# A graph layer on one core: ACT, not SP, issues the loads of the weights and of the last nodes

## The chip, the cores and the metric

The kernel runs on one core of a Trainium2 chip. The metric is the device time in microseconds of one execution, the median of several runs.

## What is computed

N is 5000 nodes, F is 64 features, everything in float32. `x` is [5000, 64], `adj` is [5000, 5000] (100 MB, mostly zeros but stored in full), `fc_w` is [64, 128].

```
h = jnp.maximum(_layernorm(x, axis=-1), 0.0)
neighbors = (adj @ h) / (num_neighbors[:, None] + 1e-7)
out = x + relu(concatenate([h, neighbors], -1) @ fc_w.T + fc_b)
```

## The kernel before

The product with `adj` is reordered: the kernel first computes g = h @ (the half of `fc_w` that belongs to the neighbours), and then adj @ g, so that the large product has 64 output features. The transpose of `adj` lies in memory in three groups of columns, 5, 4 and 1 blocks of 512 (the last one shorter). `LOADS` lists 38 loads in order: group by group, and in a group 512 rows of it at a time (4 tiles of 128 rows), which in group 0 is 128 partitions of 4 x 2560 floats, that is 5,120 KB and a contiguous run of 40,960 bytes on each partition. They go into one ring in SBUF, `raw` (32,768 floats a partition). Three loads of group 0 fit in it. `load(n)` on SP waits with `load_used` until PE has used up what lay in the place.

**PE** (`tensor_program`) does in this order: waits for the bias (`bias_loaded`) and spreads it over the partitions (line 683); `turn(0)` transposes the first 1024 normalized nodes (line 576); waits for both weight loads (`weights_loaded`, 32); `weigh(0)` multiplies them with the weights (line 588); then for each load: waits for its landing, and multiplies it (line 627). A tile of group 0 is 12 matrix instructions, a load 48. A set of 8 tiles of g (`g_sb`) is needed before its rows of `adj`; `turn(b)` and `weigh(b)` for the sets 1 to 4 are put between the tiles (`TURN_AFTER`, `WEIGH_AFTER`), the first ones after tile 3 and tile 5. After the last tile of a load `load_used` goes up.

**DVE** clears the parts of tiles that transfers don't fill (`x_cleared`, `weights_cleared`), and then normalizes the nodes in five sets of 8 tiles. The last set needs `x_loaded[1]`, two transfers of the last nodes. Between `normalize(1)` and `normalize(2)` stands `add_bias(0)`, which waits for the bias.

**ACT** warms its table for the square root, then issues `load_few` (the bias, and the few last nodes from partition `PAD0` = 96 on), then the squares and roots of the layer norm, and the copies `ht` and `g_sb` out of PSUM. After the second set it issues the neighbour counts, `load_counts`. It issues on a DMA queue of its own, q10 in the profile; SP's is q1 and POOL's q0.

**POOL** clears `bias_row`, `ones` and other tiles, and loads the eight remaining rows of `adj` (`adj_rem`).

**SP** issues x in two halves (line 257), the tail of x (96 partitions of 1 KB, line 262), waits for `weights_cleared`, issues the weights twice, once for each half of the partitions (line 266, 128 runs of 256 bytes each), and then the 38 loads (line 253). Each load has a semaphore of its own, out of 24.

Of the kernel before, what the change touches and what calls it, by code (L numbers as in the profile page):

```python
# [39 lines left out]
def gnn_layer(nc, x, adj_groups, num_neighbors, fc_t, fc_b, out):  # L40
# [9 lines left out]
    N, F = x.shape  # L50
# [11 lines left out]
    PAD0 = LAST_LANES // 32 * 32  # L62
# [27 lines left out]
    def place(n):  # L90

        g, m, i0, _ = LOADS[n]
        return (RING[g][1] + m * RUN + i0) % RING[g][0] * WIDTH[g]

    def place_end(n):
        return place(n) + (LOADS[n][3] - LOADS[n][2]) * WIDTH[LOADS[n][0]]

    def loads_before(n):

        over = [k + 1 for k in range(n) if place(k) < place_end(n) and place(n) < place_end(k)]  # L100
        return max(over + [n - LANDINGS + 1, 0])
# [13 lines left out]
    with ExitStack() as ctx:  # L115
        def sb(name, shape, dt=F32):
            return ctx.enter_context(nc.sbuf_tensor(name, shape, dt))

        def sem(name):
            return ctx.enter_context(nc.semaphore(name))  # L120
# [3 lines left out]
        x_sb = sb("x_sb", [LANES, TILES, F])  # L124
# [15 lines left out]
        w_both = sb("w_both", [2 * F, 2, 2 * F])  # L140
# [20 lines left out]
        x_loaded = [sem("x_loaded_main"), sem("x_loaded_last")]  # L161
        nn_cleared = sem("nn_cleared")
        nn_loaded = sem("nn_loaded")
        weights_cleared = sem("weights_cleared")
        weights_loaded = sem("weights_loaded")
# [34 lines left out]
        def flat(v):  # L200
            return v.rearrange("p t f -> p (t f)")
# [5 lines left out]
        def tail(v):  # L207

            return v[0:LAST_LANES, ROWS:TILES, :].rearrange("p t f -> p (t f)")

        def tail_nodes(v):
            return v[TAIL0:N, :].rearrange("(p t) f -> p (t f)", t=RUN)
# [22 lines left out]
        def weighed_parts(k, part):  # L235

            return y[k][:].rearrange("p (i s q f) -> p i s q f", i=2, s=2, q=2)[:, :, :, part, :]
# [4 lines left out]
        def loaded(n):  # L242
            return landed[n % LANDINGS], 16 * (n // LANDINGS) + 16

        def sync_program(sp):
            def load(n):
                g, m, i0, i1 = LOADS[n]
                w = WIDTH[g]
                if loads_before(n):
                    sp.wait_ge(load_used, loads_before(n))  # L250
                r = RUN if m < FULL else TAIL_RUN
                rows = adj_groups[g][m * BLOCK:m * BLOCK + r * LANES, 0:w].rearrange("(p i) c -> p (i c)", i=r)
                sp.dma_start(raw[:, place(n):place_end(n)], rows[:, i0 * w:i1 * w]).then_inc(loaded(n)[0], 16)  # L253

            def load_x(k):
                r = slice(ROWS // 2 * k, ROWS // 2 * (k + 1))
                sp.dma_start(x_sb[:, r, :], x[0:TAIL0, :].rearrange("(p r) f -> p r f", r=ROWS)[:, r, :]  # L257
                             ).then_inc(x_loaded[0], 16)

            load_x(0)  # L260
            load_x(1)
            sp.dma_start(tail(x_sb)[0:PAD0], tail_nodes(x)[0:PAD0]).then_inc(x_loaded[1], 16)  # L262
            sp.wait_ge(weights_cleared, 1)
            for s in range(2):
                k = slice(s * F, (s + 1) * F)
                sp.dma_start(w_both[k, s, :].rearrange("r (k c) -> r k c", k=2), fc_t.rearrange("(k r) c -> r k c", k=2)  # L266
                             ).then_inc(weights_loaded, 16)
            for n in range(len(LOADS)):
                load(n)

            sp.wait_ge(out_ready, LAST)
            sp.dma_start(out[0:TAIL0, :].rearrange("(p r) f -> p (r f)", r=ROWS), flat(out_sb[:, 0:ROWS, :])
                         ).then_inc(stored, 16)
            sp.wait_ge(stored, 16)
# [44 lines left out]
        def scalar_program(act):  # L319
            def load_few():  # L320

                act.wait_ge(bias_cleared, 1)
                act.dma_start(bias_row[0:1, :], fc_b.rearrange("(a f) -> a f", a=1)).then_inc(bias_loaded, 16)
                act.wait_ge(x_cleared, 1)
                act.dma_start(tail(x_sb)[PAD0:LAST_LANES], tail_nodes(x)[PAD0:LAST_LANES]).then_inc(x_loaded[1], 16)

            def load_counts():
                act.wait_ge(nn_cleared, 1)
                act.dma_start(nn[:, 0:ROWS], num_neighbors[0:TAIL0].rearrange("(p r) -> p r", r=ROWS)
                              ).then_inc(nn_loaded, 16)  # L330
                act.dma_start(nn[0:LAST_LANES, ROWS:TILES],
                              num_neighbors[TAIL0:N].rearrange("(p t) -> p t", t=RUN)).then_inc(nn_loaded, 16)

            def ln_square(b):
                act.wait_ge(ln_dve, LN_OPS * b + 3)
                nc.scalar.activation(sums[0][:], cen[:], ACT.Square).then_inc(ln_act, 1)  # L336

            def ln_std(b):
                act.wait_ge(ln_dve, LN_OPS * b + 5)
                nc.scalar.activation(std[:], var[:], ACT.Sqrt).then_inc(ln_act, 1)  # L340

            def copy_turned(b):
                act.wait_ge(turned_done, b + 1)
                if b >= 2:
                    act.wait_ge(weighed, b - 1)
                if b == SETS - 1:
                    act.wait_ge(rem_cleared, 2)

                    k = turned[HALF:LANES, :].rearrange("k (t p) -> k p t", t=RUN)[:, 0:LAST_LANES, :]
                    nc.scalar.activation(ht_rows[HALF:LANES, :].rearrange("k (p t) -> k p t", t=RUN), k, ACT.Copy)  # L350

                    nc.scalar.activation(
                        ht_rem[HALF:LANES, 0:REM * REM_STEP].rearrange("k (p t z) -> k p t z", t=RUN, z=REM_STEP)[:, :, :, 0],
                        k[:, LAST_LANES - REM // RUN:LAST_LANES, :], ACT.Copy)
                nc.scalar.activation(ht[b % 2][:], turned[:], ACT.Copy).then_inc(turned_copied, 1)  # L355

            def copy_g(b):
                act.wait_ge(weighed, b + 1)
                to = g_sb[:, BT * b:BT * (b + 1), :].rearrange("p (s i) f -> p i s f", s=2)
                for k in range(2):  # L360
                    nc.scalar.activation(to[:, 2 * k:2 * k + 2, :, :], weighed_parts(k, 1), ACT.Copy).then_inc(g_copied, 1)  # L361

            def copy_spread(b):
                act.wait_ge(spread_done, b + 1)
                w = BLOCK if b != ALONE else BLOCK // 2 + SIDE
                nc.scalar.activation(rnn_bc[:, b, 0:w], y[b % 2][:, 0:w], ACT.Copy).then_inc(spread_copied, 1)  # L366


            act.wait_ge(warm_ready, 1)
            nc.scalar.activation(std[:, 0:1], warm[:], ACT.Sqrt)  # L370
            load_few()
            for b in range(SETS):
                ln_square(b)
                ln_std(b)
                if b == 0:
                    copy_turned(0)
                else:
                    copy_g(b - 1)
                    copy_turned(b)
                if b == 1:  # L380
                    load_counts()
            copy_g(SETS - 1)
            for b in range(SETS):
                copy_spread(b)
            act.wait_ge(out_ready, LAST + 1)
            act.dma_start(tail_nodes(out), tail(out_sb)).then_inc(last_stored, 16)
            act.wait_ge(last_stored, 16)
# [181 lines left out]
        def tensor_program(pe):  # L569
# [142 lines left out]
            flip_last()  # L712

        sync_program(nc.sync)
        gpsimd_program(nc.gpsimd)
        scalar_program(nc.scalar)
        vector_program(nc.vector)
        tensor_program(nc.tensor)
# [27 lines left out]
```

## Time and profile before

| | |
|---|---|
| time, median of 3 runs | 246.38 us (246.18 to 246.43) |
| the profiled execution's own time | 246.37 us |
| span of the profile, first to last instruction | 244.9 us |
| PE busy | 202.8 us (83%) |
| DVE, ACT, POOL busy | 41.6, 15.1, 6.7 us |
| moved by DMA | 102.79 MB, mean 420 GB/s |
| chain that ended last | DMA 67%, PE 18%, issue 11% |

The profile is of one execution. Times in it count from its first instruction. PE is TensorE, DVE VectorE, ACT ScalarE, POOL GpSimd; SPq, ACTq and POOLq are the instructions that issue transfers. A DMA share of 1 means that all 16 engines had a packet in hand; large packets are counted in the window in which they begin, so a short window may show more than 1.

### The profile page before, as it was taken

How to read it: one execution, taken by the hardware profiler on the slowest of the kernel's cores; microseconds unless marked ns; L12 is line 12 of the kernel's file. 1: busy time of each engine (PE TensorE's matmuls, PEld its weight loads, DVE VectorE, ACT ScalarE, POOL GpSimd, SP SyncE). 2: the span in 40 equal slices, each digit the busy share in tenths (PEclk: the TensorE clock that was granted, in tenths of full speed). 3: DMA queues.
4: the chain of work that ended last, by engine and by line, in shares of the span. 5: the costliest groups of instructions: out<-in, count | busy, mean ns of one | idle time of the engine just before them, and what ended most of it. 6: DMA issues, size and time to landing. Idle time of an engine off the chain costs nothing.

```text
span 244.9 us, 2438 instructions
## 1 busy us (share of the span) xinstructions
PE 202.8 (83%) x1086; PEld 84.6 (35%) x1086; DVE 41.6 (17%) x102; ACT 15.1 (6%) x34; POOL 6.7 (3%) x18
## 2 busy tenths in 40 slices
PE   0168789997969796998799899898896699888995
PEld 0143234342324332453233333342222233133663
DVE  1752033304400200050000530221000000002311
ACT  2130201201200110010000300000000000000000
POOL 6000100000100000000000000000000000000000
PEclk9999979999999999999999999999999999999999
DMA  9899999999999999999999999999999999999997
GB/s 305 363 435 435 442 420 408 429 428 442 440 429 448 428 438 435 442 435 415 399 437 428 428 431 434 428 428 439 420 439 434 412 431 426 416 421 419 417 405 283
DMA packets 6847, 102.79 MB, mean 420 GB/s; under 512 B 1346, under 2 KB 1934, under 8 KB 3638
## 3 DMA queue, kind: packets, MB, share of 16 engines
q1 hardware_dynamic: 6304, 102.37, 98.4%
q8 instruction: 8, 0.13, 0.2%
q10 hardware_dynamic: 374, 0.12, 0.2%
q0 software_dynamic: 160, 0.16, 0.2%
q14 instruction: 1, 0.01, 0.0%
HBM read 101.37 MB, written 1.28 MB: 419 GB/s over the span
## 4 chain that ended last, share of the span: by engine, by line
DMA 67%; PE 18%; issue 11%; DVE 2%; SPq 2%; DVEq 0%
DMA raw<-adj_group 67%; PE acc L627 16%; DVE rnn_diag L475 1%; PE turned L627 1%; PE y L613 1%; SPq L266 1%; SPq L253 1%; SPq L257 0%; PE y L605 0%; PE turned L576 0%; DVE out_sb L538 0%; DVE rnn_diag L483 0%; DVE rnn_diag L480 0%; SPq L262 0%; PE acc L677 0%
## 5 line engine op out<-in xcount | busy, mean ns | idle before, releaser
L627 PE MATMUL acc<-raw,g_sb 128*64 128x512 f32 (+1 forms) x780 | 157.2, 556 | 26.0 <-DMA raw<-adj_group 26.0
L627 PEld LDWEIGHTS acc<-raw,g_sb 128*64 128x64 f32 x780 | 55.4, 138 | 123.3 <-issue 84.1
L627 PE MATMUL turned<-raw,g_sb 128*64 128x196 f32 x156 | 15.4, 341 | 1.0 <-DMA raw<-adj_group 0.9
L446 DVE TENSOR_TENSOR out_sb<-y,bias 128x128 f32<-128x128 f32 x20 | 4.4, 282 | 55.0 <-ACT g_sb L361 55.0
L504 DVE TENSOR_TENSOR sums<-acc,rnn_bc 128x512 f32<-128x512 f32 x4 | 2.6, 685 | 60.1 <-PE acc L627 58.1
L588 PE MATMUL y<-w_both,ht 128*128 128x256 f32 (+1 forms) x40 | 12.1, 441 | 0.8 <-ACT ht L355 0.8
L627 PEld LDWEIGHTS turned<-raw,g_sb 128*64 128x64 f32 x156 | 10.0, 134 | 6.5 <-DMA raw<-adj_group 4.1
L588 PEld LDWEIGHTS y<-w_both,ht 128*128 128x128 f32 x40 | 8.0, 217 | 3.9 <-issue 2.7
L576 PE MATMUL turned<-ident,h_pairs 128*128 128x128 f32 x20 | 3.7, 315 | 5.1 <-DVE h_pairs L434 5.1
L530 DVE TENSOR_TENSOR out_sb<-y,out_sb 128x512 f32<-128x512 f32 (+1 forms) x5 | 3.2, 638 | 23.4 <-PE y L659 20.2
L422 DVE TENSOR_REDUCE var<-sums 128x8 f32<-128x512 f32 x5 | 3.4, 686 | 19.9 <-ACT sums L336 19.9
L361 ACT ACTIVATE g_sb<-y 128x256 f32<-128x256 f32 x10 | 3.3, 381 | 53.7 <-PE y L588 35.0
L683 PE MATMUL acc<-bias_row,ones 128*128 128x64 f32 x2 | 0.7, 448 | 5.8 <-DMA bias_row<-fc_b 5.8
L475 DVE TENSOR_TENSOR rnn_diag<-ident,rnn 128x512 f32<-128x512 f32 x8 | 5.1, 686 | 0.2 <-PE y L613 0.2
L613 PE MATMUL y<-rnn_diag,ones 128*64 128x512 f32 (+1 forms) x20 | 4.6, 552 | 0.5 <-DVE rnn_diag L475 0.4
L366 ACT ACTIVATE rnn_bc<-y 128x512 f32<-128x512 f32 (+1 forms) x5 | 2.9, 588 | 31.6 <-PE y L613 31.6
L480 DVE TENSOR_TENSOR rnn_diag<-ident_twice,rnn 128x256 f32<-128x256 f32 x1 | 0.4, 426 | 25.6 <-issue 25.6
L576 PEld LDWEIGHTS turned<-ident,h_pairs 128*128 128x128 f32 x20 | 2.4, 156 | 6.8 <-issue 6.8
L355 ACT ACTIVATE ht<-turned 128x512 f32<-128x512 f32 x5 | 3.0, 597 | 23.9 <-PE turned L576 23.9
L411 DVE TENSOR_REDUCE mean<-x_sb 128x8 f32<-128x512 f32 (+1 forms) x6 | 3.4, 587 | 4.9 <-DMA x_sb<-x 4.9
L646 PE MATMUL acc<-adj_rem,g_sb 128*64 128x512 f32 (+1 forms) x20 | 4.2, 550 | 0.0
L290 POOL DMA_DIRECT2D adj_rem<-adj_group x2 | 1.3, 650 | 86.2 <-PE acc L646 61.2
(61 smaller groups left out, 48.9 us busy)
## 6 DMA issues: line engine op xcount, KB each, us to landing
raw<-adj_group SPq DMA_DIRECT2D x9, 5120.0 KB, 27.3
raw<-adj_group SPq DMA_DIRECT2D x7, 4096.0 KB, 27.9
raw<-adj_group SPq DMA_DIRECT2D x4, 2048.0 KB, 29.2
raw<-adj_group SPq DMA_DIRECT2D x7, 784.0 KB, 26.2
raw<-adj_group SPq DMA_DIRECT2D x1, 3840.0 KB, 24.5
raw<-adj_group SPq DMA_DIRECT2D x3, 1024.0 KB, 26.7
raw<-adj_group SPq DMA_DIRECT2D x4, 392.0 KB, 18.9
x_sb<-x SPq DMA_DIRECT2D x2, 576.0 KB, 4.8
```

The source lines that it names most:

```text
L355: nc.scalar.activation(ht[b % 2][:], turned[:], ACT.Copy).then_inc(turned_copied, 1)
L361: nc.scalar.activation(to[:, 2 * k:2 * k + 2, :, :], weighed_parts(k, 1), ACT.Copy).then_inc(g_copied, 1)
L411: last = nc.vector.tensor_reduce(narrow(mean[:]), rows, AX_X, ALU.add)
L422: nc.vector.tensor_reduce(var[:], sums[0][:].rearrange("p (t f) -> p t f", f=F), AX_X, ALU.add).then_inc(ln_dve, 1)
L446: last = nc.vector.tensor_tensor(to[:, 2 * k:2 * k + 2, :], weighed_parts(k, 0)[:, :, s, :], bias[:].unsqueeze(1).to_broadcast([LANES, 2, ...
L475: last = nc.vector.tensor_tensor(split(to[:, s, :]), ident[:].unsqueeze(1).to_broadcast(shape), rnn[:, m + s:ROWS:FULL].unsqueeze(2).to_br ...
L530: nc.vector.tensor_tensor(o, split(y[b % 2][:, 0:RUN * F * (m1 - m0)]), o, ALU.add).then_inc(summed, 1)
L576: last = nc.tensor.transpose(turned[:, c], h_pairs[b % 2][:, c], ident[:])
L588: last = nc.tensor.matmul(weighed_tiles(i)[:, 0:w], ht[b % 2][:, c:c + LANES], flat(w_both[:])[:, 0:w], start=True, stop=True)
L613: last = nc.tensor.matmul(y[b % 2][k, c], ones[:, 0:HALF], r, start=True, stop=True, tile_position=(0, s * HALF))
L627: last = nc.tensor.matmul(acc[b][s * HALF:(s + 1) * HALF, 0:width], g_sb[:, t, :], k, start=g < G - 1 and t == 0, stop=t == CH - 1, tile_p ...
L646: last = nc.tensor.matmul(acc[b][s * HALF:(s + 1) * HALF, 0:width], g_sb[:, CH, :], k, start=g == G - 1, stop=False, tile_position=(0, s * ...
```

## The change

The issue of the tail of x and of the two weight loads goes from SP to ACT, into `load_few`, ahead of the bias and the few last nodes. `load_few` itself goes ahead of ACT's first activation, before which its table is loaded. SP issues the loads of `raw` right behind x. Nothing is computed otherwise.

```diff
--- before.py
+++ after.py
@@ -259,12 +259,6 @@
 
             load_x(0)
             load_x(1)
-            sp.dma_start(tail(x_sb)[0:PAD0], tail_nodes(x)[0:PAD0]).then_inc(x_loaded[1], 16)
-            sp.wait_ge(weights_cleared, 1)
-            for s in range(2):
-                k = slice(s * F, (s + 1) * F)
-                sp.dma_start(w_both[k, s, :].rearrange("r (k c) -> r k c", k=2), fc_t.rearrange("(k r) c -> r k c", k=2)
-                             ).then_inc(weights_loaded, 16)
             for n in range(len(LOADS)):
                 load(n)
 
@@ -319,6 +313,13 @@
         def scalar_program(act):
             def load_few():
 
+
+                act.dma_start(tail(x_sb)[0:PAD0], tail_nodes(x)[0:PAD0]).then_inc(x_loaded[1], 16)
+                act.wait_ge(weights_cleared, 1)
+                for s in range(2):
+                    k = slice(s * F, (s + 1) * F)
+                    act.dma_start(w_both[k, s, :].rearrange("r (k c) -> r k c", k=2),
+                                  fc_t.rearrange("(k r) c -> r k c", k=2)).then_inc(weights_loaded, 16)
                 act.wait_ge(bias_cleared, 1)
                 act.dma_start(bias_row[0:1, :], fc_b.rearrange("(a f) -> a f", a=1)).then_inc(bias_loaded, 16)
                 act.wait_ge(x_cleared, 1)
@@ -366,9 +367,9 @@
                 nc.scalar.activation(rnn_bc[:, b, 0:w], y[b % 2][:, 0:w], ACT.Copy).then_inc(spread_copied, 1)
 
 
+            load_few()
             act.wait_ge(warm_ready, 1)
             nc.scalar.activation(std[:, 0:1], warm[:], ACT.Sqrt)
-            load_few()
             for b in range(SETS):
                 ln_square(b)
                 ln_std(b)
```

## Rows read from the trace of the kernel before

**Rows 1.** Page, span in forty slices: DMA share in tenths, GB/s of each slice.
```profile
DMA  9899999999999999999999999999999999999997
GB/s 305 363 435 435 442 420 408 429 428 442 440 429 448 428 438 435 442 435 415 399 437 428 428 431 434 428 428 439 420 439 434 412 431 426 416 421 419 417 405 283
```

**Rows 2.** Chain that ended last, in order of time: start, length, what.
```profile
4.67 40.31 DMA raw<-adj_group
...
45.02 8.84 PE acc L627 x48
```

**Rows 3.** Waits of SP's queue: total us, times, longest.
```profile
SPq L253 <- PE acc L627: 198.4, 23, 23.2
```

**Rows 4.** Page, DMA queues: packets, MB, share of 16 engines.
```profile
q1 hardware_dynamic: 6304, 102.37, 98.4%
...
q10 hardware_dynamic: 374, 0.12, 0.2%
```

**Rows 5.** Timeline, 0 to 22 us: start, busy us, engine, line, operation.
```profile
0.74 1.28 ACT L370 ACT_TABLE_LOAD   x1 [0.74 <-PEq L739]
...
0.75 0.85 SPq L257 DMA_DIRECT2D x_sb<-x  x2
...
1.37 0.27 DVE L392 MEMSET w_both<- 128x256 f32 x1
...
1.60 0.52 ACTq L323 DMA_DIRECT2D bias_row<-fc_b  x1
...
1.65 0.42 SPq L262 DMA_DIRECT2D x_sb<-x  x1
...
2.12 1.40 SPq L266 DMA_DIRECT2D w_both<-fc_t  x2
...
3.56 1.55 SPq L253 DMA_DIRECT2D raw<-adj_group  x3
...
5.81 0.69 PE L683 MATMUL acc<-bias_row,ones 128*128 128x64 f32 x2 [5.81 <-DMA bias_row<-fc_b]
...
8.28 0.63 ACT L336 ACTIVATE sums<-cen 128x512 f32<-128x512 f32 x1 [6.04 <-DVE cen L418]
...
11.65 1.09 PE L576 MATMUL turned<-ident,h_pairs 128*128 128x128 f32 x4 [5.15 <-DVE h_pairs L434]
...
13.51 3.75 PE L588 MATMUL y<-w_both,ht 128*128 128x256 f32 x8 [0.78 <-ACT ht L355]
...
17.30 0.66 ACT L361 ACTIVATE g_sb<-y 128x256 f32<-128x256 f32 x2 [2.25 <-PE y L588]
...
19.42 2.80 PE L627 MATMUL acc<-raw,g_sb 128*64 128x512 f32 x14 [2.16 <-DMA raw<-adj_group]
```

**Rows 6.** Two windows: busy us by engine, clock, DMA share, GB/s.
```profile
1.50:2.00 0.50, 0.00 (x0) 0.00 (x0) 0.19 (x2) 0.50 (x1) 0.50 (x3) 1.00 1.09 120
2.00:3.00 1.00, 0.00 (x0) 0.00 (x0) 0.00 (x0) 0.23 (x2) 1.00 (x1) 1.00 0.62 152
```

**Rows 7.** DMA queues in the window 2 to 5 us.
```profile
q1 hardware_dynamic: 224, 0.96, 87.2%
```

**Rows 8.** Timeline, 28 to 34 us.
```profile
28.87 0.36 ACTq L329 DMA_DIRECT2D nn<-num_neighbors  x1
```

**Rows 9.** DMA queues in the window 29 to 32.5 us.
```profile
q1 hardware_dynamic: 58, 1.72, 114.1%
```

**Rows 10.** DMA queues in the window 32.5 to 34 us.
```profile
q1 hardware_dynamic: 15, 0.61, 95.5%
...
q10 hardware_dynamic: 16, 0.00, 0.9%
```

**Rows 11.** DMA queues in the window 32.5 to 57 us.
```profile
q10 hardware_dynamic: 256, 0.02, 0.8%
```

**Rows 12.** Timeline of PE, 34 to 140 us.
```profile
37.48 1.99 PE L588 MATMUL y<-w_both,ht 128*128 128x256 f32 x8
```

**Rows 13.** DMA issues by line: count, KB each, median us to landing.
```profile
adj_rem<-adj_group POOLq DMA_DIRECT2D x1, 16.0 KB, 11.7
```

## The prediction

> **What bounds the kernel now.** I read the page's forty slices first, then the chain that ended last, then the waits of SP's queue, and then the opening in small windows. The slices show the 16 DMA engines at nine tenths or more in nearly all of them, at 400 to 448 GB/s after the first two [rows 1]. The chain's longest piece is a load of `raw` in flight for 40.3 us; then 8.84 us of multiplications free its place in the ring [rows 2]. That isn't PE setting the pace: SP waited 198.4 us in all for PE to free places [rows 3] while the engines stayed full with the two loads behind. Three loads of 5,120 KB fit in the ring, one takes about 12.2 us, and PE uses one up in 8.8 us. So the kernel ends when the last byte of `adj` has come. A stall of PE costs nothing until all queued loads have landed; time in which the DMA engines are dry goes one for one to the end. The question is when they start and whether they ever run dry.
>
> **How the queues are served.** The page counts 6304 packets on q1 (SP's queue) and 374 on q10 (ACT's) [rows 4]. I can rebuild both from the program with one packet per contiguous row plus one completion packet per engine used. SP: 38 loads x 144 = 5472, x 288, tail 112, weights 288, output 144: 6304. ACT: counts 144 + 112, bias 2, last nodes 4, last store 112: 374. So a load of `raw` is eight 40,960-byte rows per engine, and the two weight loads are 288 packets: per engine 8 rows of 256 B, a completion, 8 rows, a completion, that is 18 packets.
>
> A row of 40,960 B takes one engine 1.53 us: 102.37 MB in 98.4% of 16 x 244.9 us [rows 4] is 26.6 GB/s an engine, 1.54 us, and the 435 GB/s slices [rows 1] give 1.51.
>
> Small packets of another queue have to be fitted between these. The trace has exactly that case. ACT issues the neighbour counts (256 packets, 16 an engine, some 20 KB) at 28.87 us [rows 8]. From 29 to 32.5 us q10 moves nothing [rows 9]. From 32.5 to 34 us it moves 16 packets beside 15 of q1 [rows 10], one an engine in the time of one big row. Its 256 packets need until the window that ends at 57 us [rows 11]: 24 us for 20 KB. The same shows on POOL's queue, where 16 KB took 11.7 us to land [rows 13]. So on each engine a small queue gets one packet for each packet of SP's, and before the first it waits for what is already lined up.
>
> The Trainium skill (DMA: Bandwidth & Descriptors, Queues, rings and completion order) says the same of the turn, that an engine goes round its queue rows packet by packet, and adds that a packet typically holds 9 to 17 descriptors. By that addition 16 weight rows would go in one or two turns and the change would be nearly free; the trace has one row per packet for these shapes.
>
> **The change, part by part.**
>
> *Removed from SP.* Tail 0.42 us and weights 1.40 us of issue [rows 5]. The first load of `raw` is issued at 1.65 us in place of 3.56, 1.9 us earlier. This isn't 1.9 us of gain, since the engines are busy with x by then. From 2 to 5 us q1 moved 0.96 of x's 1.18 MB [rows 7], so x drains at about 5.4 us, and `raw` rows only stand behind it. What can be gained is idle DMA at the start: a share of 0.62 in the window from 2 to 3 us [rows 6], 0.4 us, if the tail fills them; the weights arrive too late for it. Bounds 0 to 0.5 us of gain (tail and weights, 0.16 MB, are 0.4 us of DMA at 435 GB/s wherever they go); I take 0.3.
>
> *Added to ACT ahead of its table.* Tail at about 0.74 us (0.42), a wait for the weights' clearing (DVE ends it at 1.64 [rows 5]), weights until about 3.1, bias (0.5) until 3.7, last nodes 0.25, then table 1.28 and the warm square root 0.2: done near 5.5. ACT's first real work is at 8.28 [rows 5]. The cover is 2.8 us, so this costs nothing. Behind the wait stand the bias and last nodes, which go out 1.5 us later than now.
>
> *Where the weights stand now.* Before, they were in front of `raw` on the same queue. Now x and the first loads of `raw` are on SP's queue and the weights on ACT's. SP issues `raw` at 1.65, ACT the first weights at about 1.69, while most of x is still queued. In the old trace the bias, issued on ACT at 1.60, has no packet on q10 before 5 us [rows 7], so what arrives then stands behind x. The weights and the first `raw` rows come up together at about 5.4 us and take turns: 18 for the weights, then two for the bias, on one engine. PE waits for the bias first, then for the weights.
>
> A turn is 8/9 of 1.53 us, as every ninth packet of SP is a tiny completion: 1.36 us. Nineteen turns after the first are 25.9 us. The first comes at 5.4 us, or up to 2.6 us later if rows of `raw` are already lined up: the counts waited 3.6 us from issue to the first packet [rows 8, 9], x only about 1.0 [rows 5, 6]. I take half, 1.3, and 0.7 us from the bias's last packet to PE (now PE starts at 5.81 and q10 has no packet before 5 us, so it is at most 0.8 [rows 5, 7]): 5.4 + 1.3 + 25.9 + 0.7 = 33.3, rounded up to 33.5 because the counts' pace was nearer 1.5 us a turn. Bounds 32.0 (nothing ahead) and 36.7 (2.6 ahead at 1.5 us a turn).
>
> *What that does to PE.* Bias product 0.7 us; then from `turn(0)` to the second `g_sb` copy as now, 11.65 to 17.96 us [rows 5], 6.3. DVE and ACT have x ready long before. The first multiplication starts at 33.5 + 7.0 = 40.5 us, in place of 19.42 [rows 5]. Load 0 is used up at 40.5 + 8.8 = 49.3 [rows 2], and only then may SP issue the fourth. Its first packet comes 1.0 us later, at 50.3.
>
> *When the engines run dry.* Three loads are 24 rows an engine, 36.7 us; from 5.4 us, with 0.4 for tail and weights, they end at 42.5. Dry from 42.5 to 50.3: **7.8 us**. No second gap follows: after load 0 PE needs a transposition (some 0.6 us), 8.8 of load 1 and a warm `weigh` of 1.99 [rows 12], 11.4 us, under the 12.2 of the fourth load. This margin is 0.8 us; at half clock that `weigh` takes what `weigh(0)` takes, 3.75 us [rows 5], and 1 us more is lost.
>
> *Sum.* 7.8 - 0.3 = +7.5 us on the profiled execution of 246.37 (span 244.9 and 1.5 around it), which is the median of 246.38: **253.9 us**.
>
> **Rivals.**
>
> A. *The weights pass ahead of `raw`.* If they reach the engines before the first `raw` rows and are taken in at once, or several rows move per turn, or they mix with x's 0.18-us packets, PE starts early enough. The point where it decides: load 0 must be used up by 42.5 - 1.0 = 41.5, so the bias must be seen by 41.5 - 8.8 - 7.0 = 25.7 us, six turns before my figure. For it: ACT's weight issue may begin nearly with SP's, and x is slow until 3 us [rows 6]. Against it: x was wholly lined up in front of the bias, and the counts show one row per turn. Then the time is 246.4 less 0 to 0.5: 246.2. Chance 0.08, nearly all inside 0.2%.
>
> B. *The earlier issue counts* (the other side). With A's condition met, the engines take `raw` 1.9 us earlier in effect or at least fill their 0.5 us idle at the start: 244.5 to 245.9, centre 245.7. The idle share up to 3 us speaks for it, the full share after that against. Chance 0.04.
>
> C. *The same mechanism, larger or smaller.* A few weight rows pass with x, each worth 1.36 us: 248.5 to 251.2 with two to four of them. Or a cold TensorE: if first multiplications run at the 1.2 GHz level, 2 us more, and the second gap 1 us: 257. This is the range of my forecast; its chance with the forecast is 0.88.
>
> **How the numbers follow.** Forecast with C 0.88, all slower; A 0.08; B 0.04. 0.2% of this kernel is 0.5 us, about what can be told from no change. Slower 0.88, same 0.08, faster 0.04. The early bias (32.0) gives 252.4 and the late one (36.7) 257.1; three to four passed weight rows take the low end to 249.0, and the second gap with a late bias the high end to 258.0. A and B are left outside.
>
> **What the new profile would show.** Right: q10 with about 16 packets per 1.5 us from 6 us on; the bias product near 33.5 us and the first product of line 627 near 40.5 (lines as in the kernel before); the weights' landing some 25 to 29 us after issue instead of 4.7; two DMA slices of the forty well below the rest around 43 to 50 us; no idle DMA after that. Wrong: a bias product before 26 us, or DMA slices full throughout. If PE starts at 40 us but the DMA slices stay full, the ring is deeper than I count; if the gap is there but the end doesn't move, the kernel isn't DMA-bound later on.

## The result: 4% slower, and what the profile after shows

The changed kernel takes 256.36 us (median of 6 runs, 255.3 to 257.35), the kernel before 246.31 (median of 6 beside it). The ratio is 1.0405, with a 95% interval of 1.0388 to 1.0423: 10.05 us slower. The forecast was 253.9, in a range of 249.0 to 258.0. The profiled execution took 257.12 us, with a span of 255.7.

Line numbers after line 262 have moved: 627 is now 628, 588 is 589, 576 is 577, 683 is 684.

The page first: its DMA shares and GB/s in forty slices of 6.4 us, where before all slices were full [rows 1], and the packet counts of the queues [rows 4].

```profile
DMA  7999994099999999999999999999999999999996
GB/s 303 413 413 445 458 436 205 0 354 433 418 429 408 438 436 449 419 423 423 445 430 432 420 426 428 446 420 426 438 436 431 418 426 420 423 415 418 420 404 260
...
q1 hardware_dynamic: 5904, 102.20, 94.2%
q10 hardware_dynamic: 774, 0.29, 0.5%
```

The eighth slice, from 44.8 to 51.1 us, moves nothing at all, and the seventh half of what it could. 400 packets have gone from q1 to q10: 112 of the tail and 288 of the weights, as counted.

The timeline from the start, up to the first multiplication of `raw` (compare [rows 5]):

```profile
0.76 0.40 ACTq L317 DMA_DIRECT2D x_sb<-x  x1
...
1.65 49.76 SPq L253 DMA_DIRECT2D raw<-adj_group  x4
1.67 1.37 ACTq L321 DMA_DIRECT2D w_both<-fc_t  x2
3.08 0.73 ACTq L324 DMA_DIRECT2D bias_row<-fc_b  x1
...
4.13 1.28 ACT L372 ACT_TABLE_LOAD   x1 [4.13 <-issue]
...
33.56 0.69 PE L684 MATMUL acc<-bias_row,ones 128*128 128x64 f32 x2 [33.56 <-DMA bias_row<-fc_b]
...
34.05 1.06 PE L577 MATMUL turned<-ident,h_pairs 128*128 128x128 f32 x4
```

```profile
35.89 3.75 PE L589 MATMUL y<-w_both,ht 128*128 128x256 f32 x8 [0.78 <-ACT ht L356]
40.48 10.57 PE L628 MATMUL acc<-raw,g_sb 128*64 128x512 f32 x48 [0.84 <-ACT g_sb L362]
50.98 0.66 PE L577 MATMUL turned<-ident,h_pairs 128*128 128x128 f32 x4
```

SP issues `raw` 1.9 us earlier, as meant, and ACT's table load hides. But PE sits from the start until 33.56 us for a bias of 256 bytes. Its first multiplication of `raw` is at 40.48 us in place of 19.42, and SP can issue the fourth load only after that of load 0 has ended:

```profile
51.08 0.33 SPq L253 DMA_DIRECT2D raw<-adj_group  x1
```

Windows of the same execution (busy us by engine, granted clock, DMA share, GB/s; a packet counts where it begins):

```profile
41.00:42.00 1.00, 1.00 (x4) 0.27 (x2) 0.93 (x4) 0.00 (x0) 0.00 (x0) 1.00 0.67 287
42.00:51.00 9.00, 9.00 (x47) 3.57 (x43) 0.57 (x1) 0.00 (x0) 0.00 (x0) 1.00 0.00 0
51.00:52.00 1.00, 1.00 (x8) 0.59 (x8) 0.00 (x0) 0.33 (x1) 0.00 (x0) 1.00 0.00 0
52.00:53.00 1.00, 1.00 (x8) 0.38 (x6) 0.00 (x0) 0.72 (x2) 0.65 (x1) 1.00 2.26 655
```

No row of `adj` begins between 42 and 52 us. PE is busy in all of it, on data that landed long ago.

What kept the bias is in the queues' packets. First the window 6.5 to 8 us, then 6.5 to 29 us (queue, packets, MB, share):

```profile
q1 hardware_dynamic: 16, 0.66, 101.3%
q10 hardware_dynamic: 16, 0.00, 1.2%
```

```profile
q1 hardware_dynamic: 255, 9.79, 101.7%
q10 hardware_dynamic: 255, 0.06, 1.2%
```

255 packets against 255: one small packet for each packet of SP's. In 22.5 us ACT's queue moves 0.06 MB. It is the pattern of the neighbour counts [rows 9 to 11], at the place where it hurts.

The chain that ended last says it too (start, length, what): where SP's issue and a load stood at its beginning, there is now the bias.

```profile
1.67 0.65 ACTq L321
2.36 0.68 ACTq L321
3.08 30.44 DMA bias_row<-fc_b
33.56 0.69 PE acc L684 x2
34.26 0.87 PE turned L577 x4
```

### The profile page after: what moved, and what is told of

Read it like the earlier page. It is cut to its first block, busy times and chain, and to the rows that moved or that the text cites. A ratio compares the mean times of both kernels' runs of the same rounds, so it can differ in the third digit from the quotient of the medians.

```text
span 255.7 us, 2438 instructions
## 1 busy us (share of the span) xinstructions
PE 205.8 (80%) x1086; PEld 86.0 (34%) x1086; DVE 41.6 (16%) x102; ACT 15.1 (6%) x34; POOL 6.6 (3%) x18
## 4 chain that ended last, share of the span: by engine, by line
DMA 47%; PE 37%; issue 12%; DVE 2%; ACTq 1%; ACT 0%; SPq 0%; DVEq 0%
DMA raw<-adj_group 35%; PE acc L628 30%; DMA bias_row<-fc_b 12%; PE y L589 4%; PE turned L577 1%; DVE rnn_diag L476 1%; PE turned L628 1%; PE y L614 1%; ACTq L321 1%; PE acc L684 0%; PE y L606 0%; ACT g_sb L362 0%; ACT ht L356 0%; DVE out_sb L539 0%; DVE rnn_diag L484 0%
## 5 line engine op out<-in xcount | busy, mean ns | idle before, releaser
L628 PE MATMUL acc<-raw,g_sb 128*64 128x512 f32 (+1 forms) x780 | 160.7, 567 | 11.2 <-DMA raw<-adj_group 10.4
L628 PEld LDWEIGHTS acc<-raw,g_sb 128*64 128x64 f32 x780 | 56.9, 140 | 110.2 <-issue 89.3
L423 DVE TENSOR_REDUCE var<-sums 128x8 f32<-128x512 f32 x5 | 3.4, 686 | 41.5 <-ACT sums L337 41.5
## 6 DMA issues: line engine op xcount, KB each, us to landing
raw<-adj_group SPq DMA_DIRECT2D x1, 3840.0 KB, 25.4
```

What stands on the lines that cost most here:

```text
L423: nc.vector.tensor_reduce(var[:], sums[0][:].rearrange("p (t f) -> p t f", f=F), AX_X, ALU.add).then_inc(ln_dve, 1)
L628: last = nc.tensor.matmul(acc[b][s * HALF:(s + 1) * HALF, 0:width], g_sb[:, t, :], k, start=g < G - 1 and t == 0, stop=t == CH - 1, tile_p ...
```

## The experiments

Each kernel is a small edit of the changed one (e7 of the kernel before) and its time is the median of the runs of its own comparison; ratios are to runs of the kernel before on the same chip. Lines of the edits that only move or repeat others are shortened to `...`.

### e1: the tail alone on ACT's queue

```diff
-            for n in range(len(LOADS)):
+            sp.wait_ge(weights_cleared, 1)
+            for s in range(2):
+                ...
+                sp.dma_start(w_both[k, s, :]..., fc_t...).then_inc(weights_loaded, 16)
+            for n in range(len(LOADS)):
...
-                act.wait_ge(weights_cleared, 1)
-                for s in range(2):
-                    ...
-                    act.dma_start(w_both[k, s, :]..., fc_t...).then_inc(weights_loaded, 16)
```

> One part alone: the tail of x goes to ACT, the weights stay on SP behind x. Turn-taking theory: the weights are again in front of raw on the same queue, so nothing waits; 246.0 to 246.5 us, bias product near 5.8 us. If instead anything ahead of ACT's table or two queues at the start are what costs, several us of the 10 must show here.

Measured 246.3 us, ratio 1.0003 (0.9994 to 1.0012); the bias product starts at 6.38 us. The tail costs nothing on ACT's queue, and gives nothing back: the gain of 0.3 us that the forecast took for idle DMA at the start isn't to be seen in the time.

### e2: the weights alone on ACT's queue

```diff
             load_x(1)
+            sp.dma_start(tail(x_sb)[0:PAD0], tail_nodes(x)[0:PAD0]).then_inc(x_loaded[1], 16)
...
-                act.dma_start(tail(x_sb)[0:PAD0], tail_nodes(x)[0:PAD0]).then_inc(x_loaded[1], 16)
```

> The other part alone: the weights go to ACT, the tail stays on SP, which delays the first issue of raw by 0.45 us and puts seven small packets an engine between x and raw. Turn-taking theory: some seven to nine weight packets get past before the first raw row, so the bias is seen 10 to 12 us earlier (21 to 24 us) and the DMA engines do not run dry: 246.3 to 248 us. Rival, that the weights on ACT's queue cost the same wherever raw stands: 256.

Measured 249.32 us (247.17 to 250.35), ratio 1.0107 (1.0056 to 1.0158). In the median that misses the expectation (246.3 to 248) and is far below the rival's 256. In the profiled run, the fastest, the bias is seen at 22.33 us, inside the expectation, because six packets an engine of ACT's queue get past before `raw` fills it; the window 5 to 6.5 us, where the changed kernel has none of q10:

```profile
q1 hardware_dynamic: 164, 0.86, 165.0%
q10 hardware_dynamic: 99, 0.02, 7.5%
```

With the bias there, PE waited another 1.76 us for the weights, which lie on all 16 engines where the bias lies on one, and load 0 took long:

```profile
25.64 3.78 PE L589 MATMUL y<-w_both,ht 128*128 128x256 f32 x8 [1.76 <-DMA w_both<-fc_t]
30.25 11.23 PE L628 MATMUL acc<-raw,g_sb 128*64 128x512 f32 x48 [0.84 <-ACT g_sb L362]
```

The tail on SP's queue, with 0.45 us of delay in the first issue of `raw`, is worth 7 us of time in the median. The slower runs of this kernel weren't profiled. That fewer packets got past in them is likely, and not shown.

### e3: the bias ahead of the weights

```diff
+                act.wait_ge(bias_cleared, 1)
+                act.dma_start(bias_row[0:1, :], ...).then_inc(bias_loaded, 16)
                 act.wait_ge(weights_cleared, 1)
                 for s in range(2):
                     ...
-                act.wait_ge(bias_cleared, 1)
-                act.dma_start(bias_row[0:1, :], ...).then_inc(bias_loaded, 16)
```

> As the changed kernel, but ACT issues the bias ahead of the weights. Turn-taking theory: bias seen near 5.8 us, turn(0) near 11; the weights have 17 turns after their first, so they are seen at 30 to 31, first multiplication near 35.3, engines dry for about 5 us in place of 10: 250 to 252 us. Rival, that PE is late because of its own backlog and not because of the order in ACT's queue: 256, no change.

Measured 250.94 us (250.74 to 252.37), ratio 1.0187 (1.017 to 1.0204). PE's timeline:

```profile
6.11 0.69 PE L684 MATMUL acc<-bias_row,ones 128*128 128x64 f32 x2 [6.11 <-DMA bias_row<-fc_b]
11.29 1.09 PE L577 MATMUL turned<-ident,h_pairs 128*128 128x128 f32 x4 [4.49 <-DVE h_pairs L435]
31.30 3.78 PE L589 MATMUL y<-w_both,ht 128*128 128x256 f32 x8 [18.93 <-DMA w_both<-fc_t]
35.92 10.61 PE L628 MATMUL acc<-raw,g_sb 128*64 128x512 f32 x48 [0.84 <-ACT g_sb L362]
```

The bias comes at 6.11 us, and now it is the weights that PE waits for, until 31.30. PE's own backlog is no cause; the order in ACT's queue decides what it waits for.

### e4: half the weight packets, same bytes

```diff
-    act.dma_start(w_both[k, s, :].rearrange("r (k c) -> r k c", k=2),
-                  fc_t.rearrange("(k r) c -> r k c", k=2)).then_inc(weights_loaded, 16)
+    act.dma_start(w_both[k, s, :], fc_t[:, :]).then_inc(weights_loaded, 16)
...
-    arrays["fc_t"] = np.ascontiguousarray(np.asarray(L0_gnn_fc_w).T)
+    arrays["fc_t"] = np.ascontiguousarray(np.asarray(L0_gnn_fc_w).T.reshape(2, f, -1).transpose(1, 0, 2).reshape(f, -1))
```

> As the changed kernel, with the weights laid out in memory so that each partition takes one run of 512 B in place of two of 256 B: same bytes, half the packets (4 and a completion for each load and engine). Packet theory: 8 turns fewer, 10.9 us, bias seen near 22.7 us, multiplication near 29.6, no dry time: 246.0 to 246.7 us. If bytes or the number of transfers set the delay, bias still near 33.5 us and 256.

Measured 246.53 us (246.24 to 247.65), ratio 1.0013 (0.9999 to 1.0026). The bias is seen at 21.65 us:

```profile
21.65 0.69 PE L684 MATMUL acc<-bias_row,ones 128*128 128x64 f32 x2 [21.65 <-DMA bias_row<-fc_b]
...
28.57 11.02 PE L628 MATMUL acc<-raw,g_sb 128*64 128x512 f32 x48 [0.84 <-ACT g_sb L362]
```

Eight packets an engine fewer bring it 11.9 us earlier (33.56 - 21.65), 1.49 us each, and 32 KB a load are the same 32 KB. Packets are what is paid for. PE's first multiplication is at 28.57 us, 9 us later than in the kernel before, and the time is the same: that is the slack which the ring gives.

### e5: half the row of `raw` for the first three loads

```diff
-STEPS = [(4, 4, 4, 4, ...
+STEPS = [(2, 2, 2, 4, ...
```

> As the changed kernel, but the first 12 tiles of adj are loaded two tiles at a time: rows of 20,480 B in place of 40,960. Turn-taking theory: a turn is half as long (0.68 us), bias seen at 19 to 21 us, no dry time: 246.0 to 246.8 us. If the small queue simply waits for a number of bytes or for the first loads to land, the bias is still seen near 33 us and the time is 255 or more.

Measured 246.7 us, ratio 1.0017 (1.0008 to 1.0027). The bias product starts at 20.33 us, and from 6.5 to 18 us the queues move

```profile
q1 hardware_dynamic: 243, 4.65, 96.2%
q10 hardware_dynamic: 241, 0.06, 2.3%
```

about the packets of the changed kernel's 22.5 us in half the time. A turn is as long as SP's packet. The smaller loads also free their places sooner, so it is the bias's moment that tests the turns here, and not the time.

### e6: SP waits for the weights

```diff
+            sp.wait_ge(weights_loaded, 32)
             for n in range(len(LOADS)):
```

> As the changed kernel, but SP waits for the weights to land before it issues raw. The weights stay on ACT's queue and ahead of the table; only their meeting with raw is gone. Turn-taking theory: weights and bias seen by 7 us; the price is the dry time until raw's first packet, 1.6 to 2.3 us: 247.8 to 248.8 us. If ACT's queue or its order is the cause, 256 or more.

Measured 248.57 us, ratio 1.0094 (1.0079 to 1.0109), the bias product at 6.67 us. ACT's queue carries the weights as fast as SP's did when nothing meets them: they land 4.6 us after issue, against 4.7 before and 17.2 and 29.0 in the changed kernel. The 2.3 us are the idle engines while SP waits.

### e7: only the order of ACT's loads and its table

```diff
+            load_few()
             act.wait_ge(warm_ready, 1)
             nc.scalar.activation(std[:, 0:1], warm[:], ACT.Sqrt)
-            load_few()
```

> The kernel before, with ACT's bias and last nodes issued ahead of its table, and no transfer moved from SP. The table lies in the 6 us that ACT waits for x anyway: 246.2 to 246.5 us, no change. If the late table matters, slower by up to 1.3 us.

Measured 246.22 us, ratio 0.9999 (0.9989 to 1.0008). The table's place costs nothing.

### e8 and e9: TensorE at work before the bias lands

```diff
+            pe.wait_ge(ident_ready, 1)
+            for k in range(200):
+                nc.tensor.transpose(turned[:, 0:LANES], ident[:], ident[:])
             pe.wait_ge(bias_loaded, 16)
```

> As the changed kernel, with 200 extra transposes of the unit matrix into turned before PE waits for the bias (their result is overwritten and not used), so that TensorE's clock is at its higher level when the bias lands. Theory: the 2.6 us by which the forecast was short come from load 0 at the lower level (10.57 us in place of 8.8). Then weigh(0) takes 2.0 in place of 3.75 us and load 0 8.8 us, and the time falls by 3.5 to 4 us to 252 to 253.5 us, with all runs close together. Rival, that the shortfall is a second gap later on or a slow restart of the DMA engines: at most 0 to 1 us less.

Measured 256.01 us (255.04 to 257.68), ratio 1.0403 (1.0352 to 1.0453): neither. The transposes ended at 25.4 us and PE idled again. `weigh(0)` was slow as ever, but in the profiled run, of 255.04 us, load 0 was not.

```profile
1.52 23.88 PE L684 MATMUL turned<-ident 128*128 128x128 f32 x200 [1.52 <-POOL ident L292]
33.83 0.69 PE L687 MATMUL acc<-bias_row,ones 128*128 128x64 f32 x2 [8.42 <-DMA bias_row<-fc_b]
...
36.15 3.59 PE L589 MATMUL y<-w_both,ht 128*128 128x256 f32 x8 [0.78 <-ACT ht L356]
40.58 8.81 PE L628 MATMUL acc<-raw,g_sb 128*64 128x512 f32 x48 [0.84 <-ACT g_sb L362]
```

e9 has 265 of them.

> As the changed kernel, with 265 extra transposes before the wait for the bias in place of 200 (result not used). With 200 they ended at 25.4 us, PE then idled 8.4 us and the granted clock fell to half again. 265 should end between 32 and 33.5 us, just ahead of the bias. Clock theory: weigh(0) 2.0 us in place of 3.75, load 0 8.8 in place of 10.57, multiplication from about 38.7, load 0 used up at 47.5, and the time near 253.3 us (252.5 to 254) with little spread, against the changed kernel's 255.3 to 257.35. Rival, that the shortfall against the forecast and the spread of two us have nothing to do with TensorE's clock: 255 to 257 again, with weigh(0) short or not.

Measured 255.73 us (254.2 to 256.19), ratio 1.0367 (1.0341 to 1.0394). The expected 253.3 isn't reached, and the interval overlaps that of the changed kernel. The bias product and `turn(0)` are fast (0.43 and 0.61 us, against 0.69 and 1.06), but `weigh(0)` is still slow:

```profile
33.59 0.43 PE L687 MATMUL acc<-bias_row,ones 128*128 128x64 f32 x2 [1.60 <-DMA bias_row<-fc_b]
33.87 0.61 PE L577 MATMUL turned<-ident,h_pairs 128*128 128x128 f32 x4
35.25 3.53 PE L589 MATMUL y<-w_both,ht 128*128 128x256 f32 x8 [0.78 <-ACT ht L356]
39.62 8.81 PE L628 MATMUL acc<-raw,g_sb 128*64 128x512 f32 x48 [0.84 <-ACT g_sb L362]
```

The windows of this run show why: the granted clock (third number from the end) fell after all, to its lower level of 1.2 GHz.

```profile
30.00:34.00 4.00, 2.40 (x23) 2.17 (x22) 0.00 (x0) 0.00 (x0) 0.00 (x0) 1.00 1.13 483
35.00:38.00 3.00, 2.75 (x7) 2.24 (x8) 1.96 (x5) 0.83 (x3) 0.00 (x0) 0.50 1.01 437
39.00:44.00 5.00, 4.38 (x26) 2.18 (x28) 2.34 (x7) 0.47 (x2) 0.00 (x0) 1.00 0.65 279
```

As a treatment both failed. What they are good for is the pair e8 and changed kernel: multiplication starts at 40.58 and 40.48 us, load 0 takes 8.81 and 10.57 us, and the times are 255.04 and 257.12.

### e10: one more load ahead of the bias

```diff
+        scratch = sb("scratch", [F, 2 * F])
...
+                act.dma_start(scratch[:].rearrange("r (k c) -> r k c", k=2), fc_t...).then_inc(scratch_loaded, 16)
                 act.wait_ge(bias_cleared, 1)
                 act.dma_start(bias_row[0:1, :], ...).then_inc(bias_loaded, 16)
```

> As the changed kernel, with one more load of the same 128 runs of 256 B on ACT's queue, between the weights and the bias, into a tile that nothing reads: 32 KB more. Turn-taking theory: nine more turns, 12.3 us (16.6 of them at most), bias seen near 45.8 us, and as the DMA engines are dry already, all of it goes to the end: 267 to 270 us. Rival, that the delay of the bias is a wait for the three queued loads to pass: bias and end later by 2 us or less.

Measured 265.89 us (264.91 to 267.09), ratio 1.0784 (1.0756 to 1.0813): 9.5 us more than the changed kernel for 32 KB that nobody reads. The bias is seen at 43.44 us, 9.9 later in place of 12.3, and the time is just below the 267 us expected. The expectation overlooked that `raw` itself ends: in the window from 42 to 43.5 us q10 has 37 packets and q1 only 16 completions, so the last small packets have nothing to alternate with and go at once. The rival's 2 us are out of the question.

### e11 and e12: the changed kernel again

> The changed kernel once more, unchanged, for another profile of it. Its times fell in two groups, 255.3 to 255.6 and 257.1 to 257.35 us, and its one profile is of the second, with load 0 taking 10.57 us. Clock theory: a run of the first group shows load 0 at 8.8 to 9 us, a run of the second at 10.5 or more, with the bias seen near 33.5 in both. Rival: the groups differ in when the bias comes (a packet more or less ahead of it, 1.5 us), with load 0 the same.

> The same again, a second look: load 0 at 8.8 to 9 us if the time is near 255.5, 10.5 or more if it is near 257.2; the bias near 33.5 us in both.

They took 255.29 and 255.41 us, with the bias seen at 33.90 and 33.91 and load 0 in 8.81 us. The row of e11:

```profile
40.42 8.81 PE L628 MATMUL acc<-raw,g_sb 128*64 128x512 f32 x48 [0.84 <-ACT g_sb L362]
```

So, as far as three profiles show it (one of them of the slower group), the two groups of times are the two lengths of load 0, and not a packet more or less ahead of the bias, which came within 0.35 us of the same moment.

That this length is TensorE's clock can be read from the products themselves. These are the first 3.58 us of load 0, in the changed kernel's profile and then in e11's (the count in brackets is of matrix instructions):

```profile
40.48:44.06 3.58, 3.58 (x10) 1.23 (x12) 1.00 0.43 183
40.42:44.00 3.58, 3.58 (x20) 1.70 (x22) 1.00 0.43 183
```

Half as many fit. The clock readings kept in the trace begin, at the higher level, at 44.06 us in the changed kernel's profile, inside load 0, and at 39.05 in e11's and 40.25 in e12's, ahead of it. 3.58 us at half speed lose 1.8 us, and load 0 took 1.76 more. The same holds for e3 (first reading at 39.59 us), e10 (54.51), e4 (33.06) and e2 (35.16): 8.8 us and half of the time from the start of load 0 to that reading give 10.6, 10.9, 11.0 and 11.3, where 10.61, 10.86, 11.02 and 11.23 were measured. Why the higher level comes sooner in one execution than in the next isn't shown.

## Why the prediction was right, and by what it was short

**The mechanism held in each step.** The weights and the bias stand in turn with `raw` (e4, e5, and 255 packets against 255); the bias was forecast at 33.5 us and seen at 33.56 to 33.91; the first multiplication at 40.5 and seen at 40.42 to 40.83. The engines ran dry near 42.5, as forecast, and in place of 50.3 began again at 52 in the changed kernel's profile; in e11, where load 0 took 8.81 us, they began in the window from 50 us:

```profile
50.00:51.00 1.00, 1.00 (x6) 0.29 (x4) 0.00 (x0) 0.72 (x2) 0.46 (x1) 1.00 2.07 614
```

Two small things in the forecast don't hold as written. The second weight load landed 29.0 us after its issue, inside the 25 to 29 named, but the first already after 17.2. And the late bound of the bias, 5.4 + 2.6 + 19 x 1.5 + 0.7, is 37.2 us and not 36.7; nothing came near it.

**Of the rivals**, A (weights pass ahead) doesn't happen in this kernel, but its condition is real: e2, e4 and e5 meet it or come near it. With the bias at 20 to 22 us e4 and e5 lose less than 0.2% in the median. But its point of decision, a bias at 25.7 us, was set too late: e2 had the bias at 22.33 us and still lost 1 us in its fastest run and 1.1% in the median. The forecast reckoned with 7.0 us from the bias to the first multiplication and 8.8 for load 0; e2 took 7.92 and 11.23, so that load 0 was used up at 41.48, just at the forecast's limit of 41.5. B (the earlier issue counts) is out: e1 and e4, where nothing runs dry, aren't faster than before. The rule of the Trainium skill (DMA: Bandwidth & Descriptors, Queues, rings and completion order) holds in its turn by packets. Its 9 to 17 descriptors a packet don't describe these weight loads, which took a turn for each run of 256 B; e4 shows it. The same page's advice that issuing from several engines only saves issue time (Issuing engines are not separate DMA queues) fits as far as the saving goes: 1.9 us were saved at the issue, and the kernel ended 10 us later.

**What goes one for one to the end.** For the eight profiled runs in which the fourth load had to wait past the end of the third, or just to it, I add start and length of load 0's multiplications and compare with the run's own time:

| run | load 0 used up, us | time, us | difference |
|---|---|---|---|
| after | 40.48 + 10.57 = 51.05 | 257.12 | 206.07 |
| e2 | 30.25 + 11.23 = 41.48 | 247.17 | 205.69 |
| e3 | 35.92 + 10.61 = 46.53 | 252.37 | 205.84 |
| e8 | 40.58 + 8.81 = 49.39 | 255.04 | 205.65 |
| e9 | 39.62 + 8.81 = 48.43 | 254.20 | 205.77 |
| e10 | 50.35 + 10.86 = 61.21 | 267.09 | 205.88 |
| e11 | 40.42 + 8.81 = 49.23 | 255.29 | 206.06 |
| e12 | 40.83 + 8.81 = 49.64 | 255.41 | 205.77 |

Over 20 us the difference stays within 0.42. In e4 and e5, where load 0 was used up at 39.59 and 37.92 us and nothing ran dry, it is 206.8 and 208.7: up to 39.59 us the moment cost next to nothing. So the moment at which the fourth load may be issued decides the time, and all before it only through that moment. The forecast was 49.3 and 253.9, a difference of 204.6.

**The sizes that were off.** The step "load 0 is used up at 40.5 + 8.8" was right for e11 and e12 and short by 1.8 us for the profiled run: with PE idle until the bias, the slow stretch that before fell on `weigh(0)` and a later load reached into load 0 in some executions. Rival C had priced it at 2 us. The other part is the sum after it, for the profiled run 206.07 against 204.6, 1.5 us. Two pieces of that can be read.

The first sixteen rows of the fourth load are slow: the window 52 to 53 us above has a share of 2.26 for 0.655 MB, which is 16 rows of 40,960 bytes, so 2.26 us a row in place of 1.53, 0.7 us more. The long idle time isn't needed for that. In e2 the engines hardly stopped (14 rows of 1.53 us began between 41 and 42 us), and 11 rows of the fourth load, which began from 42.4 to 43 us, took 2.2 us each:

```profile
41.00:42.00 1.00, 1.00 (x11) 0.45 (x7) 0.00 (x0) 0.00 (x0) 0.00 (x0) 1.00 1.33 573
42.40:43.00 0.60, 0.60 (x6) 0.23 (x4) 0.00 (x0) 0.32 (x2) 0.20 (x1) 1.00 2.53 751
```

The other piece is work that had been moved beside the first three loads before and now comes after the dry time: the rows of `adj_rem` and part of the neighbour counts. In the kernel before they take 1.6% (q0) and 0.6% (q10) of the 15 us from 28 to 43 us, 0.3 us. Together that is 1.0 of the 1.5 us. What makes up the other 0.5 isn't shown. The gain of 0.3 us at the start may be a part: it was forecast, and e1 and e4, where it should stand alone, don't show it in the time.

## What to carry to other kernels

A small transfer on a queue of its own isn't ahead of a stream on another queue, but in step with it: count its packets (one for each contiguous run and a completion an engine), multiply with the time of one packet of the stream, and see who waits for the last. Put what the pipeline waits for first on the stream's own queue ahead of the stream, or in fewer, longer runs; and before moving an issue, ask whether the transfer engines had been idle at that moment. A deep ring of loads forgives a late consumer up to a point, here between a first multiplication at 28.57 us (e4, no loss to speak of) and at 30.25 (the profiled run of e2, 1 us; at 35.92 in e3 it is 4.7 us in the median), and from there each microsecond goes to the end.

## What the runs showed of the hardware

- `raw` issued 0.45 us later, behind the tail's six rows an engine, took over 11 us off the wait (bias at 22.33 us in the profiled run of e2, 33.56 in the changed kernel).
- In the changed kernel the tail's 1 KB packets, issued at 0.76 us, took turns with x's at once (112 packets of q10 from 2 to 5 us), while before, the bias, issued at 1.60 us, had none before 5 us [rows 7].
- Eight products of `weigh(0)` took 3.75 us, where 1.99 is usual, in windows for which the profile of the changed kernel gives a granted clock of 1.00. Its trace has no clock reading before 44.06 us; ahead of the first reading the column says 1.00 whatever the level was, and the durations have to be read.
- The first rows of a load that was issued when the engines had nothing or hardly anything left took 2.1 to 2.4 us each in place of 1.53 (windows of the changed kernel, e2, e10, e11 and e12), after 10 us of idle engines and after next to none.
- e9's clock was at half from 35 to 38 us, although PE had worked from 1.5 to 32 us and had idled only for gaps of 1.6 and 0.8 us since.
